# Turns of four columns, counts loaded per cell, ScalarE-cleared PSUM, one wait and one operand moved in a four-layer graph network

## The reference

```python
def sage_mean(x, w_self, w_neigh, b):
    summed = segment_sum(x[src], dst, N)
    return x @ w_self + (summed / maximum(deg, 1)[:, None]) @ w_neigh + b

x = layernorm(x + relu(concat([x, mean over dst of x[src]]) @ W.T + b))
# layer 1: messages from both ends of an edge, with the edge's own features
x = layernorm(x + layer_norm(leaky_relu(agg / counts) + x))
#          agg = segment_sum of H[src] @ Wf.T + E @ We.T + b, and of the same backwards
# layer 2: two attention convolutions (4 heads)
#          e = leaky(s_src[src] + s_dst[dst]); alpha = exp(e - max over dst) / sum over dst
#          out = segment_sum(alpha * h[src], dst)
x = layernorm(x + gat(relu(gat(x))) + x @ Wr + br)
# layer 3: h = sage(relu(sage(x))); keep the top quarter of the rows by a score, zero the rest
x = layernorm(x + sage(relu(sage(h where kept))))
```

## Time and profile before

| | us |
|---|---|
| median of 3 runs | 9576.34 |
| lowest and highest | 9571.98, 9588.64 |
| the profiled execution, its own time | 9587.65 |
| its span | 9585.9 |
| sorting stage, first to last scatter | 232.5 to 1440.6 |
| count-matrix loops | 1530 to 2872, 2872 to 3536 |
| attention stage | 5128 to 7635 |

### The profile page before, as it was taken

How to read it: one execution, slowest core, us unless ns; L and a number is a source line. 1 busy time by engine, 2 the same in 40 slices (tenths; PEclk the granted TensorE clock), 3 DMA queues, 4 the chain that set the end, 5 groups by cost and what they waited for, 6 DMA issues and landing times. The chain is left out here.

```text
span 9585.9 us, 155347 instructions
## 1 busy us (share of the span) xinstructions
PE 6694.3 (70%) x40260; PEld 4514.2 (47%) x40299; DVE 4673.7 (49%) x12985; ACT 1515.5 (16%) x2248; POOL 3457.7 (36%) x3459
## 2 busy tenths in 40 slices
PE   0366404666666657999995777767777679986999
PEld 0355302434333224555554666656666635544555
DVE  6877715555554442222226777767777721113011
ACT  1222101111111111010002333322232200000000
POOL 0777775555553200000005666646666500000000
PEclk6788656676766668999997999989999989997999
DMA  0222101222221304677772222212222156654666
GB/s 15 52 69 72 40 2 57 76 79 74 69 75 62 57 38 139 172 185 175 185 185 53 49 48 48 48 45 48 48 47 48 38 148 190 190 156 115 190 193 182
DMA packets 871577, 901.11 MB, mean 94 GB/s; under 512 B 421540, under 2 KB 820227, under 8 KB 864868
## 3 DMA queue, kind: packets, MB, share of 16 engines
q1 hardware_dynamic: 753541, 637.16, 24.4%
q0 software_dynamic: 109664, 179.92, 8.7%
q10 hardware_dynamic: 8064, 80.29, 2.0%
HBM read 722.84 MB, written 93.87 MB: 85 GB/s over the span
## 5 line engine op out<-in xcount | busy, mean ns | idle before, releaser
L1903 POOL DMA_INDIRECT d_row_ring<-table_att,src_at x1664 | 1582.0, 951 | 932.7 <-issue 476.7
L2412 PE MATMUL psum<-e_a_ring,e_parts 128*128 128x448 bf16 x8232 | 1579.1, 353 | 84.0 <-DVE e_parts L2494 84.0
L786 PE MATMUL psum<-b_hot 128*128 x2860 | 892.0, 456 | 1039.7 <-DVE b_hot L958 954.5
L769 POOL DMA_INDIRECT b_row_ring<-edge_attr,b_entry x896 | 883.8, 986 | 978.5 <-SPq L747 738.5
L2412 PEld LDWEIGHTS psum<-e_a_ring,e_parts 128*128 128x128 bf16 x8232 | 806.7, 98 | 825.7 <-issue 90.0
L786 PEld LDWEIGHTS psum<-b_hot 128*128 x2860 | 316.4, 111 | 1560.3 <-issue 1434.2
L352 POOL DMA_INDIRECT listed<-a_record,a_slot_no x832 | 933.1, 1122 | 318.6 <-issue 275.9
L1928 PE MATMUL psum<-edges_out,edges_in 128*128 128x120 f32 x4896 | 756.9, 319 | 176.5 <-ACT edges_in L1992 156.7
L1311 PE MATMUL psum<-c_a_ring,c_parts 128*128 128x448 bf16 x4116 | 812.7, 356 | 44.5 <-DMA c_a_ring<-adjacency 39.7
L1928 PEld LDWEIGHTS psum<-edges_out,edges_in 128*128 128x128 f32 x4896 | 701.1, 228 | 221.1 <-DVE edges_out L2087 220.0
L956 DVE TENSOR_SCALAR b_hot<-b_iota,b_key_id (+1 forms) x1430 | 387.4, 271 | 832.8 <-issue 646.1
...
## 6 DMA issues: line engine op xcount, KB each, us to landing
...
c_a_ring<-adjacency SPq DMA_DIRECT2D x686, 224.0 KB, 2.9
...
b_row_ring<-edge_attr,b_entry POOLq DMA_INDIRECT x896
listed<-a_record,a_slot_no POOLq DMA_INDIRECT x832
...
```

The lines of the kernel that those rows point to most:

```text
L769: pool.indirect_dma_start(out=row_ring[:, u % 4, g, 0:D], out_offset=None, in_=a["edge_attr_128"], in_offset=bass.IndirectOffsetOnAxis(ap= ...
L786: mm = nc.tensor.matmul(ps[:, v, :], hot[:, at, j, 0:P].rearrange("p a f -> p (a f)"), hot[:, at, j, P + v * WIN:P + (v + 1) * WIN].rearra ...
L1903: pool.indirect_dma_start(out=row_ring[:, u % 4, g, :], out_offset=None, in_=table_att[layer], in_offset=bass.IndirectOffsetOnAxis(ap=src_ ...
L2412: mm = nc.tensor.matmul(psum[:, 2 * (turn % 2) + v, 0:WIN], parts[:, piece, s, :], a_ring[:, s % SEVEN, v * WIN:(v + 1) * WIN], start=(s = ...
```

## The change

Three edits.

1. Sorting stage: ScalarE copies the turned destinations a third time, into a PSUM bank (`dst_near`, fp32), and the one-hot `hot` (L574) reads them there, not from SBUF. VectorE waits for this copy once.
2. Count-matrix stage: a turn is four columns. The ring holds two turns, each in two halves of two columns, and the halves are signalled and waited for one by one. The length of a cell is rounded up to fours (at least one). Each cell's running count is loaded (seven words on VectorE where there was one). TensorE's cell is one loop that always accumulates (`start=False`); ScalarE clears a buffer with a copy of a tile of zeros after it has copied the cell, so `s_copied` rises by two a cell.
3. Attention stage: VectorE's wait for `s_out` in `enter` is gone; ScalarE's `widened` waits for it, but not in the first two steps of a pass.

```diff
+            dst_near = bank[3][:, 0:TC]
...
+                nc.scalar.copy(dst_near.rearrange("p (u g) -> p u g", g=G),
+                               bank[1].rearrange("p (g u) -> p u g", g=G)[:, 0:NB, :]).then_inc(s_at, 1)
...
-                    V.tensor_tensor(is_dst_b[:, h, :, :], bc(dst_at[:, bass.ds(batch * G, G)], 2, [P, G, P]),
+                    V.tensor_tensor(is_dst_b[:, h, :, :], bc(dst_near[:, bass.ds(batch * G, G)], 2, [P, G, P]),
                                     bc(iota[:, bass.ds(tile * P, P)], 1, [P, G, P]), ALU.is_equal).then_inc(s_hot, 1)
...
+                dve.wait_ge(s_at, 2)
...
-            hot = sbb("hot", [P, HOT, 2, P + WIDE], BF16)
+            hot = sbb("hot", [P, 2, HOT // 2, 2, P + WIDE], BF16)
...
+            blank = sbb("blank", [P, WIDE], BF16)
...
+                nc.gpsimd.memset(blank[:], 0.0)
...
-                    def pair(g, start):
-                        hold(pe, s_hot, at0 + g + 1, s_held_pe)
-                        at = bass.ds((at0 + g) & (HOT - 1), 1)
-                        for j in range(2):
-                            for v in range(2):
-                                mm = nc.tensor.matmul(
-                                    ps[:, v, :], hot[:, at, j, 0:P].rearrange("p a f -> p (a f)"),
-                                    hot[:, at, j, P + v * WIN:P + (v + 1) * WIN].rearrange("p a f -> p (a f)"),
-                                    start=(start and j == 0), stop=not (start and j == 0), skip_group_check=True)
-                        mm.then_inc(s_hot_free, 1)
-
-                    pair(0, True)
-                    with pe.Fori(0, n - 1) as g:
-                        pair(g + 1, False)
+                    with pe.Fori(0, n) as g:
+                        turn = pe.snap(at0 + g)
+                        four = hot[:, bass.ds(turn & 1, 1), :, :, :].rearrange("p a h j f -> p (a h) j f")
+                        for half in range(2):
+                            hold(pe, s_hot, turn * 2 + (half + 1), s_held_pe)
+                            for j in range(2):
+                                for v in range(2):
+                                    mm = nc.tensor.matmul(
+                                        ps[:, v, :], four[:, half, j, 0:P],
+                                        four[:, half, j, P + v * WIN:P + (v + 1) * WIN],
+                                        start=False, stop=True, skip_group_check=True)
+                            mm.then_inc(s_hot_free, 1)
 
                 def cells(s, first, end, before):
                     for w in range(first, end):
                         at0, then = before[w - first:w - first + 2]
-                        n = nc.s_assert_within(pe.snap(then - at0), 2, COLS // 2,
-                                               skip_runtime_bounds_check_because="a cell has from two to all column pairs")
-                        pe.wait_ge(s_copied, s * NWIDE + (last_use[w] + 1 + NWIDE))
+                        n = nc.s_assert_within(pe.snap(then - at0), 1, COLS // 4,
+                                               skip_runtime_bounds_check_because="a cell has from four to all columns")
+                        hold(pe, s_copied, s * (2 * NWIDE) + 2 * (last_use[w] + 1 + NWIDE), s_held_pe)
                         cell(ps_cell[buffer_of[w]], n, at0)
...
+                def cleared(buffer):
+                    nc.scalar.copy(buffer, blank[:].rearrange("p (v f) -> p v f", v=2)).then_inc(s_copied, 1)
+
+                for buffer in ps_cell:
+                    cleared(buffer)
+                act.wait_ge(s_copied, 3)
+                act.sem_inc(s_copied, 2 * NWIDE - 3)
...
-                        hold(act, s_hot_free, then + HOT, s_held_act)
+                        hold(act, s_hot_free, then * 2 + HOT, s_held_act)
                         nc.scalar.copy(line[:, bass.ds(s & 1, 1), w * WIDE:(w + 1) * WIDE].rearrange("p a (v f) -> p (a v) f", v=2),
                                        ps_cell[buffer_of[w]]).then_inc(s_copied, 1)
-                    act.wait_ge(s_copied, s * NWIDE + 2 * NWIDE)
+                        hold(act, s_copied, s * (2 * NWIDE) + 2 * (w + NWIDE) + 1, s_held_act)
+                        cleared(ps_cell[buffer_of[w]])
...
+                        cleared(ps_cell[0])
...
-                        hold(dve, s_hot_free, at0 + g + 1, s_held_dve)
-                        at = bass.ds((at0 + g) & (HOT - 1), 1)
-                        k = nc.s_assert_within(dve.snap(k0 + g * 2), 0, COLS - 2,
-                                               skip_runtime_bounds_check_because="k0 is at most COLS - 2 n")
-                        for j in range(2):
-                            V.tensor_scalar(hot[:, at, j, 0:P].rearrange("p a f -> p (a f)"), iota[:, bass.ds(tile * P, P)],
-                                            key_id[:, bass.ds(k + j, 1)], None, ALU.is_equal)
-                            last = V.tensor_scalar(hot[:, at, j, P:].rearrange("p a f -> p (a f)"), iota[:, window],
-                                                   key_dst[:, bass.ds(k + j, 1)], None, ALU.is_equal)
-                        last.then_inc(s_hot, 1)
-                    return dve.snap(at0 + n)
-
-                def cells(s, first, end, spans, at0):
+                        k = nc.s_assert_within(dve.snap(k0 + g * 4), 0, COLS - 4,
+                                               skip_runtime_bounds_check_because="k0 is at most COLS - 4 n")
+                        ids, ends_at = key_id[:, bass.ds(k, 4)], key_dst[:, bass.ds(k, 4)]
+                        turn = dve.snap(at0 + g)
+                        four = hot[:, bass.ds(turn & 1, 1), :, :, :].rearrange("p a h j f -> p (a h) j f")
+                        for half in range(2):
+                            hold(dve, s_hot_free, turn * 2 + (half + 1), s_held_dve)
+                            for j in range(2):
+                                c = 2 * half + j
+                                V.tensor_scalar(four[:, half, j, 0:P], iota[:, bass.ds(tile * P, P)],
+                                                ids[:, c:c + 1], None, ALU.is_equal)
+                                last = V.tensor_scalar(four[:, half, j, P:], iota[:, window],
+                                                       ends_at[:, c:c + 1], None, ALU.is_equal)
+                            last.then_inc(s_hot, 1)
+
+                def cells(s, first, end, spans, before):
                     for w in range(first, end):
-                        at0 = cell(s, slice(w * WIDE, (w + 1) * WIDE), spans[w - first], at0)
-                    return at0
...
+                        cell(s, slice(w * WIDE, (w + 1) * WIDE), spans[w - first], before[w - first])
...
                     pairs = codes(s * 4, 6)
                     spans = spans_of(dve, s * NWIDE + 3, NWIDE)
-                    at0 = befores(dve, s * NWIDE + 3, 1)[0]
+                    before = befores(dve, s * NWIDE + 3, NWIDE)
                     hots(1, pairs[2:4])
-                    at0 = cells(s, 3, NWIDE, spans, at0)
+                    cells(s, 3, NWIDE, spans, before)
                     adds(s * 2, pairs[0:2])
                     hots(0, pairs[4:6])
-                    cells(s + 1, 0, 3, spans[NWIDE - 3:], at0)
+                    cells(s + 1, 0, 3, spans[NWIDE - 3:], before[NWIDE - 3:])
                     adds(s * 2 + 1, pairs[2:4])
...
+                def widened(at, h, first=False):
                     act.wait_ge(s_hot, at + 1)
+                    if not first:
+                        act.wait_ge(s_out, at)
                     nc.scalar.copy(is_dst[:, h, :, :], is_dst_b[:, h, :, :]).then_inc(s_hot_f, 1)
...
+                            widened(base + h, h, True)
...
-                    if not first:
-                        dve.wait_ge(s_out, at)
```

54 lines of the change are left out of this document (26 added, 28 removed).

## The result

The changed kernel takes 8958.83 us (median of 4 runs, 8954.88 to 8961.59), the kernel before 9580.13 us on the same comparison: a ratio of 0.9351 [0.9335, 0.9367], 621 us less. The forecast was 8980 us in a range of 8930 to 9150.

| part | before | after | difference | forecast |
|---|---|---|---|---|
| last scatter of the sorting stage at | 1440.6 | 1369.6 | -71.0 | -65 |
| count-matrix stage, first one-hot to last leftover cell | 2117.4 | 1682.0 | -435.4 | -460 |
| its first loop, a line | 42.4 | 35.3 | -7.1 x 32 | 41.9 to 33.0 |
| its second loop, a line | 41.7 | 28.6 | -13.1 x 16 | 41.5 to 30.7 |
| layers 0 and 1 | 1493.8 | 1488.2 | -5.6 | 0 |

What follows compares the result with a forecast made beforehand. GpSimd's scatters bound the sorting stage, VectorE's sequencer the count-matrix stage, VectorE the attention stage. Edits of -65, -460 and -70 sum to -595 on 9587.65 us: 8993, forecast 8980 us since that run is 11 above the median; range 8930 to 9150.

Steps and rivals of the forecast that it cites:

- the reading of L581: Sorting stage: no scatter stretch falls on L581, which reads one PSUM operand; L574 behaving likewise gives -65 us.
- The gap between turns: Count-matrix stage, first loop: 5.3 gaps a line at 0.6 us, 3.2 us for 14.1 before: -10.9 us a line.
- GpSimd's gathers (L769): Count-matrix stage, first loop: gathers take 28.7 us a line, under 33, so they stay hidden.
- TensorE at the low clock: First loop: about a third of the lines at low clock go by TensorE, so 33.0 us a line for VectorE's 31.9.
- rival 1: Count-matrix stage: TensorE at the low clock bounds it, 312 us gained in place of 459: 9130 us; chance 0.12.
- The head: Start of a first-loop line: loading seven running counts in place of one adds 1.3 us a line on VectorE.
- The clear: Count-matrix stage: ScalarE's extra operation per cell, nearest rows 906 and 934 ns, hidden by three PSUM buffers.
- rival 3: First loop: the body grown from 252 to 265 instructions stalls at its return, +109 us: 9090 us; chance 0.05.
- the end of -94: Attention stage: far bound of edit 3's forecast gain, which was -70 us within 0 to -94.
- The cut to three quarters: Attention stage: of 89 us excess wait three quarters taken as gain, -70 us, VectorE's chain through TensorE's spread being late next.
- the floor of 0.34 us a step: Attention stage: idle time before L2082 in steps without the wait, taken for all 306 steps, leaving 89 us excess.

Runs made afterwards that it cites:

- run 9: Changed kernel with SyncE's hand-over reordered (run 3), but L574's destination keys read from SBUF again: 8873.61 us.
- run 3: Changed kernel with SyncE freeing the next unit's slot before it waits for the arrival of the unit before: 8806.49 us.
- run 8: Kernel of run 3 with one more ScalarE copy of zeros in every cell, into a tile that nothing reads: 8831.53 us.
- run 7: Kernel of run 3 with a cell's running count rebuilt by the chain of register operations, turns of four kept: 9011.08 us.
- pairs_loaded: Kernel before with edits 1 and 3 and, of edit 2, only the running counts loaded per cell, turns staying pairs: 9032.89 us.
- Run 10: Changed kernel with one more VectorE wait, on a count that always holds, at the place of the moved attention wait: 8973.39 us.

## Why the forecast was right, and where not

**Edit 1** went as worked out: -71 for -65, the mean scatter 1041 ns for "near 1040", the last wait 138 us for 145. That the whole stretch under L574 would go, and not half of it for the operand that stays in SBUF, was the reading of L581, and run 9 bears it out. The rule of the Trainium skill against a PSUM operand (VectorE: DVE Perf Modes, Why PSUM operands drop a tier) had nothing to act on: the instruction took 1225 ns, not more than before.

**Edit 2** came within 25 us by luck, through errors of opposite sign: the first loop gained 226 us and not 286, the second 209 and not 173.
- The gap between turns. The forecast took 0.6 us a turn of four on top of 2.1 us of data, 2.7 us from turn to turn, since the shortest chain had shown 0.48 us between pairs. Measured: 2.5 us. VectorE's queue works through registers while data instructions run; a pair has 1.05 us of data for some 1.6 us of register work, a four 2.1 us for 2.5. So VectorE's own pace in the first loop is 30.1 us a line, measured from head to head with the supply mended, not 31.9 (27.9 in the line shown, which has the short head and no third pair).
- The step that failed is "GpSimd's gathers (L769) take 982 + 300 ns, 8 a unit, 2.8 units a line: 28.7 us. Under 33, so they stay hidden." The sum took gathers alone and left out what SyncE does between units. With its wait a unit is 12.6 us and a line 34.9, above both VectorE and TensorE, and run 3 took 152 us off by that wait alone. The row was there: GpSimd waited 440.9 us for SyncE before. It was read as slack of an engine that is early, and part of it is a fixed price of the hand-over, at least 2.1 us a unit.
- TensorE at the low clock was given a weight that it did not have: 33.0 for 31.9, and rival 1. The mean clock went up, 0.71 to 0.86, and with supply mended to 0.94.
- The head: +1.3 forecast, 5.48 for 4.17 us in three lines of four, as said.
- The clear: 910 ns, between the bounds 906 and 934, and covered (run 8).
- No return stall at 265 instructions (rival 3), as the forecast took it; run 7 shows that it waits not far off. Bodies of 323, 462 and 489 instructions idle 2.7 to 3.5 us (once 4.8) behind the closing branch, and those of 252 and 265 do not (0.3 us). But the second loop of pairs_loaded has 349 and does not stall (0.23 us), so length alone doesn't decide. The Trainium skill (Runtime: NRT & Kernel Launch, Instruction fetch mechanics) says that a taken branch stalls when its target isn't in the window of two pages. The trace agrees in that long bodies stall; 323 beside 349 would fit if it counts where a body lies in its pages, which no run here shows.

**Edit 3** was undersized: -115.5 for -70, and beyond the end of -94. The idle time before L2082 fell from 193.3 to 75.9 us, 117.4 us, and all of it came off the end; nothing was late next. Two terms failed. The cut to three quarters had no row behind it. And the floor of 0.34 us a step was too high, since it is 0.25 us now: 306 x 0.09 = 27 us more. Run 10 splits these 27. With a wait that always holds in the same place the steps idle 86.0 us, 10 more than without it, which is the wait's own price. The other 17 are a misreading: the forecast took 0.34 us for each step from the kernel before, and two in three of the steps that idle so long there stand behind the loop's branch, the one place where a held wait leaves 0.33 us; in the other two it leaves 0.25.

The total, 8959 for 8980 us, is thus in part luck: edit 2 fell 25 us short and edit 3 ran 45 us over.
